# A bound on the indices of the experts' gathers and scatters, so that empty slots are not moved

## What is computed

```
logits = x @ gate_w.T                                   # 1792 tokens, 64 experts
topv, topi = jax.lax.top_k(logits, 8)
rw = softmax(topv)
W = zeros((N, E)).at[arange(N)[:, None], topi].set(rw)
gate, up = einsum('nh,eih->nei', x, gu_w)               # 128 + 128 columns
inter_w = silu(gate) * up * W[:, :, None]
out = einsum('nei,ehi->nh', inter_w, dp_w) + sigmoid(x @ sh_gate1_w.T) * shared(x)
x = x + tanh(g_ffn) * out
```

## Time and profile before

| | us |
|---|---|
| median of 3 runs | 1776.56 (1768.63 to 1781.8) |
| the profiled execution | 1785.47 |
| its span, first to last instruction | 1783.7 |
| the first gather starts at | 1293.4 |
| the last put starts at | 1685.0 |

### The profile page before, as it was taken

The page is one execution under the profiler, slowest core; times in us unless marked ns, Lnnn a source line. Parts: engine busy times, 40 slices in busy tenths (PEclk is TensorE's granted clock), DMA queues, the critical chain, the costliest instruction groups (busy, mean ns, idle before and its releaser), DMA issues. The chain is left out here.

```text
span 1783.7 us, 24623 instructions
## 1 busy us (share of the span) xinstructions
PE 1456.5 (82%) x7484; PEld 1170.1 (66%) x7484; DVE 1253.4 (70%) x2658; ACT 711.6 (40%) x1605; POOL 857.6 (48%) x901
## 2 busy tenths in 40 slices
PE   4689898899889989979899988988479898898600
PEld 3367687676578776658777666665268788888500
DVE  2268796389889358979737897675457677777577
ACT  1123475111167311127611115554157677677400
POOL 1078552056655025655404656221377777777500
PEclk9989999999999999989999998999689999999855
DMA  6977300354310235420034530302278899999798
GB/s 189 321 234 245 102 14 26 102 157 142 104 44 6 67 121 153 141 76 18 16 113 134 137 108 15 88 28 77 74 217 265 303 322 320 305 304 295 253 425 353
DMA packets 140412, 286.01 MB, mean 160 GB/s; under 512 B 29422, under 2 KB 64840, under 8 KB 138184
## 3 DMA queue, kind: packets, MB, share of 16 engines
q1 hardware_dynamic: 112328, 212.39, 37.2%
q0 software_dynamic: 25344, 64.69, 11.0%
q10 hardware_dynamic: 2608, 7.34, 1.4%
HBM read 218.90 MB, written 67.61 MB: 161 GB/s over the span
## 5 line engine op out<-in xcount | busy, mean ns | idle before, releaser
L1542 POOL TENSOR_TENSOR q_rope<-q_rope,q_sin 128x448 f32<-128x448 f32 x192 | 214.7, 1148 | 158.9 <-DVE q_sin L984 158.6
L1548 POOL TENSOR_TENSOR prob<-prob,row_inv 128x375 f32<-128x375 f32 x201 | 162.5, 812 | 137.3 <-DVE row_inv L1006 137.2
L680 PE MATMUL bank<-q_rope,m_w 128*128 128x448 f32 x384 | 170.7, 581 | 32.4 <-DVE q_tl L990 20.4
L1608 POOL DMA_INDIRECT parts<-y_sb,t_rows x140 | 155.0, 1107 | 51.5 <-issue 35.4
L1561 POOL DMA_INDIRECT table<-entry,pos_i x128 | 121.6, 950 | 103.9 <-DVE pos_i L1099 57.8
L1601 POOL DMA_INDIRECT x_g<-xn_dram,t_rows x140 | 142.8, 1020 | 50.5 <-issue 40.2
L984 DVE TENSOR_TENSOR q_sin<-bank,sin_q 128x448 f32<-128x448 f32 (+1 forms) x256 | 158.4, 619 | 3.9
L1340 ACT ACTIVATE prob<-bank,row_max 128x375 f32<-128x375 f32 x224 | 128.6, 574 | 40.8 <-DVE row_max L998 40.4
L705 PE MATMUL bank<-ident,prob 128*125 128x128 f32 x672 | 119.6, 289 | 26.9 <-POOL prob L1548 9.4
L680 PEld LDWEIGHTS bank<-q_rope,m_w 128*128 128x128 f32 x384 | 75.6, 203 | 98.9 <-issue 91.8
L998 DVE TENSOR_REDUCE row_max<-bank 128x1 f32<-128x375 f32 x224 | 119.5, 534 | 24.1 <-PE bank L604 23.4
(11 more groups left out here) (277 smaller groups left out, 4526.6 us busy)
## 6 DMA issues: line engine op xcount, KB each, us to landing
w_gu<-in_w_gu SPq DMA_DIRECT2D x64, 512.0 KB, 4.8
p_in<-parts SPq DMA_DIRECT2D x14, 2304.0 KB, 13.1
v_raw<-v_dram SPq DMA_DIRECT2D x80, 256.0 KB, 2.7
w_dp<-in_w_dp SPq DMA_DIRECT2D x64, 256.0 KB, 6.0
m_w<-m_dram SPq DMA_DIRECT2D x64, 192.0 KB, 2.7
wq_s0h<-wq_dram SPq DMA_DIRECT2D x24, 256.0 KB, 3.5
wq_s0l<-wq_dram SPq DMA_DIRECT2D x24, 256.0 KB, 3.6
wq_s1h<-wq_dram SPq DMA_DIRECT2D x24, 256.0 KB, 3.1
```

Of the source, the lines that this page charges most:

```text
L680: m = pe.matmul(bank[5][:, 0:GT], m_w[n % NW][:, c, :], q_rope[h % 2][:, c, :], start=(c == 0), stop=(c == QC - 1))
L1542: pool.tensor_tensor(o[:, c, :], o[:, c, :], q_sin[:, c, :], ALU.add).then_inc(s_radd, 1)
L1548: pool.tensor_tensor(prob[i][:], prob[i][:], row_inv[:, i:i + 1].to_broadcast([P, L]), ALU.mult)\
L1608: pool.indirect_dma_start(parts, bass.IndirectOffsetOnAxis(ap=t_rows[x % NROW][0:size, t, 1:2].bitcast(I32), axis=0), y_sb[x % NY][t][0:si ...
```

## The change

Both indirect DMAs of the experts carry a highest valid index, and an index above it is left out with no error. A gather leaves out slots with an index above the last token; the rows of `x_g` for them then keep what was there. So a gather carries the bound only where every row of its tiles has been filled by an earlier place with the same buffer (`filled`); place 0 to 4 and 12 to 16 gather as before. A put leaves out slots with a destination behind the real rows of `parts`, in every place. Of the 140 gathers 115 carry the bound (21 tiles of 96 rows, 30 of 128, 64 of 112), and all 140 puts do: 255 instructions. Nothing else is added, removed or moved; the loop for what doesn't fit is as it was.

```diff
+def filled(x):
+
+    return all(any(TILES[y][1] > t and TILES[y][0] >= TILES[x][0] for y in range(x % NXE, x, NXE))
+               for t in range(TILES[x][1]))
...
                     pool.indirect_dma_start(x_g[x % NXE][0:size, t, :], None, xn2_dram, bass.IndirectOffsetOnAxis(
-                        ap=t_rows[x % NROW][0:size, t, 0:1].bitcast(I32), axis=0)).then_inc(s_xg[x % NXE], 16)
+                        ap=t_rows[x % NROW][0:size, t, 0:1].bitcast(I32), axis=0),
+                        bounds_check=B * S - 1 if filled(x) else None, oob_is_err=False)\
+                        .then_inc(s_xg[x % NXE], 16)
...
                     pool.indirect_dma_start(parts, bass.IndirectOffsetOnAxis(
-                        ap=t_rows[x % NROW][0:size, t, 1:2].bitcast(I32), axis=0), y_sb[x % NY][t][0:size, :], None)\
+                        ap=t_rows[x % NROW][0:size, t, 1:2].bitcast(I32), axis=0), y_sb[x % NY][t][0:size, :], None,
+                        bounds_check=YR - 1, oob_is_err=False)\
                         .then_inc(s_put[x % NY], 16)
```

## The result

| us | before | after |
|---|---|---|
| median of 14 runs each | 1777.78 (1768.63 to 1785.01) | 1788.52 (1778.59 to 1795.34) |
| the profiled execution | 1785.47 | 1791.32 |
| its span | 1783.7 | 1789.4 |
| first gather starts at | 1293.4 | 1291.2 |
| last put starts at | 1685.0 | 1690.0 |

The ratio is 1.0058, with a 95% interval of 1.0038 to 1.0077. It lies within 1%, and inside the range; but the forecast was no difference, and there is one of some 10 us. In the two profiled executions the experts, from the first gather's start to the last put's end, took 392.5 us before and 399.7 after: 7.2 us more. The span grew by 5.7, because this execution came to the experts 2.2 us earlier.

What follows compares the result with a forecast made beforehand. POOL's instruction queue was taken to bound the experts; +5 us (bound), -5.5 (fewer rows) and -0.2 (last put) gave -1, 1784.5 us for the profiled execution. With the runs' median 8.9 us below that execution: 1776 us, range 1756 to 1829.

Steps and rivals of the forecast that it cites:

- the sum: Experts: +5 us for the bound, -5.5 for fewer rows, -0.2 for the last put, together -1 us.
- POOL's queue is the bound: Experts: POOL's instructions and fixed pauses fill 382.9 of 392.5 us, so their sum sets the end.
- Rival (2): Experts bound by transfers, POOL's long instructions being waits for rows: 16.7 us shorter, 1760 us; chance 0.08.
- Price of the bound, "+5 us": Experts' bounded gathers and puts: the comparison adds 0.02 us to each of 255 instructions, 5 us.
- Rival (1): Bounded instructions get their own check or a slower row-by-row path: 1827 us at 0.222 us each; chance 0.27.
- Fewer rows, "-5.5 us": Experts' gathers and puts: POOL writes 2733 fewer rows at 2 ns each, 5.5 us less.
- rival (4): Dropped rows are replaced by some other descriptor; DMA queue's packets and POOL's time stay: 1777 us; chance 0.04.
- Rival (3): POOL's indirect DMAs go by rows really moved, beyond 2 ns: up to 23 us less, 1754 us; chance 0.06.
- The register, "hidden under the instruction before": POOL's queue: a register for the bound is set while the previous instruction runs, so pauses stay 0.30 us.
- Stalls behind VectorE: POOL's instruction time above 0.95 us, 31.8 us in all, is stalls behind VectorE's low parts, and stays.
- The last stage's DMA share, "about 0.87": Experts' last stage: DMA share should fall from 0.91 to about 0.87 while POOL's pauses stay 0.30.
- The chances: Whole kernel, with a difference of 1% as the limit: faster 0.13, same 0.60, slower 0.27.

Runs made afterwards that it cites:

- loose_reg: The change with bounds in registers set once, at the last allocated row so nothing is left out, against the kernel before: 1787.56 us, 1.0041; repeated on a slower chip, 0.9973.
- move_only: Kernel before plus a register copy ahead of each put, no bound; the unused copy never appeared in the trace, so nothing changed: 1779.07 us, ratio 0.9988.
- reg_kinds: reg_again with two tiles of 128 rows for three of 96 in places 8 to 11, against the kernel before: 1778.21 us, ratio 0.9983.
- short_g: Kernel before, no bounds, its 115 gathers fetching 16 rows fewer each, on a slower chip: 1859.63 us, ratio 1.0027 to the kernel before.
- reg_again: The change with both bounds in registers set once at the head of POOL's program, against the kernel before: 1785.47 us, ratio 1.0035.
- no_low: Kernel before with VectorE's two big low-part subtractions cut to one column after the first places, on a slower chip: ratio 1.0014 to the kernel before.
- pool_op: Kernel before with a one-word memset on POOL ahead of each of the 140 puts, on a slower chip: ratio 0.9997 to the kernel before.
- before_again: The kernel before, unchanged, profiled on a slower chip, where the kernel before takes 1867.22 us.

## Why the prediction was nearly right, and where it failed

The time lies 12 us above the forecast of 1776 and within its range, but it moved the other way: the sum said -1 us, and the medians are 10.7 us apart. What failed is the sum's two main terms; what the prediction says of the bound of the kernel held.

**POOL's queue is the bound.** Held, on the case's kind of chip. The stage grew by 7.2 us with the DMA share of the last stage down from 0.91 to 0.84. The price of the instructions, stage by stage, from the medians of undisturbed ones: gathers 21 x 0.047 (96 rows) + 30 x 0.061 (128) + 64 x 0.055 (112) = 6.3 us, puts 36 x 0.005 + 40 x 0.02 + 64 x 0.012 = 1.8 us, together 8.1. POOL's busy time grew by 9.0 - 2.7 = 6.3 us, so the stalls, which are chance, came out 1.8 shorter; its pauses and waits grew from 392.5 - 297.8 = 94.7 to 399.7 - 304.1 = 95.6, and 6.3 + 0.9 = 7.2. `loose_reg` says the same: 6.2 us more of stage than `move_only`, with 6.3 us more of POOL's busy time. `reg_kinds` fits, but would also fit a part by TensorE's steps. Rival (2), transfers, is refuted: 5.6 MB less moved gave none of its 16.7 us, and 58.9 MB was what the prediction named.

**Price of the bound, "+5 us".** Mis-sized, at 0.02 us for each of 255, a figure that was taken and not read from a row. It is 0.05 to 0.06 for a gather and 0.005 to 0.02 for a put, 8.1 us in all. I had taken the two as one instruction; they aren't, and nothing in the rows of before could tell it. Rival (1), with 0.07 as its point of decision, wasn't far for the gathers.

**Fewer rows, "-5.5 us".** This is the term that failed. The 2 ns a row come from tiles of 96 and 128 rows, where the instruction is given fewer rows (1.3 ns by the medians of the kernel before, 934, 955 and 976 ns for gathers of 96, 112 and 128 rows; 0.9 to 1.6 in `short_g`). A row that is dropped by its index is still given to the instruction, and saves nothing: `loose_reg` and `reg_again` have the same medians, and the queue's packets stay 21248. What the instruction does with such a row the profile doesn't show. The prediction held the fact for this in rival (4), "the packets stay", and priced it as 1777 with the forecast; it belonged in the sum. With 0 in place of -5.5 and 8.1 in place of 5 the sum is +8 us and not -1; the two medians of after and before are 10.7 apart, and the interval, 6.8 to 13.7 us, holds the 8. That the time still came within 12 us of the forecast owes something to luck: both terms were small, but one had the wrong size and the other nothing behind it. Rival (3) falls for the same reason.

**The register, "hidden under the instruction before".** Right while POOL is never waiting: the pauses stay 0.30. Wrong where a put waits for its result: then the MOVE takes over the wait, and the put starts 0.79 us behind the result, not 0.28. One of them, kernel after:

```profile
1684.71 1.31 ACT L1501 ACTIVATE y_sb<-bank,t_rows 112x512 f32<-112x512 f32 x2 [0.39 <-PE bank L610]
1686.18 0.94 POOL L1616 DMA_INDIRECT parts<-y_sb,t_rows  x1 [1.91 <-ACT y_sb L1501]
```

In the case's profile there are five such puts, 5 x 0.51 = 2.6 us at most, and 1.0058 against 1.0035 for `reg_again`, measured in another set, is no separation. On kind B, with some 40 of them, it is the whole cost of the change, 0.6%. The prediction asked only what hides the MOVE, not what is late when its cover is gone.

**Stalls behind VectorE.** Held, and now shown by `no_low`, though on kind B: without the subtractions the stretched instructions are gone (longest 1.24 us, against 2.0). This speaks against what the Trainium skill ("SBUF — State Buffer", Who interferes with whom) infers, that such a subtraction doesn't hold up the writing of descriptors. The same section's rule that it contends with a GpSimd instruction that reads SBUF isn't contradicted, and the prediction left it out: an indirect DMA reads its indices from `t_rows`. Which of the two is held up no run tells.

**The last stage's DMA share, "about 0.87".** It is 0.84. The same transfers are also spread over a longer stage (205 us and not 200), which by itself makes 0.87 x 200 / 205 = 0.85.

**The chances.** They don't follow from the rivals as given: half of (2) and all of (3) make 0.04 + 0.06 = 0.10 for faster, not 0.13, and then 0.63 for the same. The outcome, within 1%, is where the most weight lay either way.

## What to carry to other kernels

When an engine's queue of instructions is the bound, price a change by what it does to those instructions, not by the transfers that it saves: here a bound with nothing left out cost as much as one with all empty rows left out. And where a constant operand needs a register, set it once: a register set in front of an instruction takes over that instruction's wait.

## What the runs showed of the hardware that I hadn't expected

- A bound costs an indirect gather 0.05 to 0.06 us and an indirect scatter 0.005 to 0.02 us of POOL's time, whether or not an index is above it.
- Left-out rows of a bounded indirect DMA keep their packets (21248 in both kernels) and move no bytes (64.51 to 58.92 MB).
- The register copy ahead of a bounded DMA holds its semaphore's wait: 0.79 to 0.82 us from the result to the put, 0.28 without it.
- A memset of 0.12 us on POOL between two indirect DMAs fits into their pause: 0.31 us with it, 0.30 without (`pool_op`).
- The same kernel took 1778 and 1781 us in two sets and 1855 to 1873 us on four other chips, nearly all of the difference in the experts (392.5 us, and 476.3 in `before_again`), with a granted clock of TensorE of 0.86 there against 0.89 to 1.00, and 53.5 us of its weight loads' idle time unexplained. No run here tells the cause.
